# Two stages and a mixture of experts on one core: key spread shared with SP, smaller routing batches, earlier overlap

## What is computed

```python
# own: attention within each sequence (8 heads of 64, one shared key/value head, three branches, gated)
x1 = layernorm(x + attn(x))
# cross: 16 heads of 8 over the context, 64 keys for each sequence
q = x1 @ Wq + bq;  k = ctx @ Wk + bk;  v = ctx @ Wv + bv
r = x1 + softmax(q_h @ k_h.T / sqrt(8)) @ v_h @ Wo + bo
x2 = layernorm(r)
# experts: 8 of them, the two best of each row
t = rmsnorm(x2) * norm_scale
logits = t @ gate_w + gate_b
w = softmax(top2(logits))
y = sum(w[e] * (swiglu(t @ mlp1_w[e] + mlp1_b[e]) @ mlp2_w[e] + mlp2_b[e]) for e in top2)
out = layernorm(x2 + y)
```

## Time and profile before

| what | value |
|---|---|
| three runs | 630.25, 633.15 and 634.72 us, median 633.15 |
| the profiled execution | 630.97 us |
| its span, first to last instruction | 629.0 us |
| busy: TensorE, VectorE, ScalarE, GpSimd | 82%, 76%, 69%, 69% of the span |
| granted clock of TensorE, mean | 0.93 of full speed |

### The profile page before, as it was taken

One profiled execution on the slowest core, in us unless ns is written; L12 is line 12 of the kernel. 1 busy time (PEld: TensorE's weight loads), 2 busy tenths in 40 slices (PEclk: granted clock), 3 DMA queues, 4 the chain that ended last, 5 costly groups with the idle time before them and its releaser, 6 DMA issues.

```text
span 629.0 us, 17434 instructions
## 1 busy us (share of the span) xinstructions
PE 517.8 (82%) x5258; PEld 405.9 (65%) x5258; DVE 478.0 (76%) x1705; ACT 432.9 (69%) x1295; POOL 435.2 (69%) x446
## 2 busy tenths in 40 slices
PE   6678888888888789999999997457677888998862
PEld 3456666666666656777767765447567888887720
DVE  3679999999998776888997896646566468897602
ACT  3789999999998768888977763225334445667703
POOL 6678889898896672665668988673566654687622
PEclk9889999999998999999999998576779889999976
DMA  2256565654542221111111111231122221623152
GB/s 71 63 209 225 213 254 194 240 167 116 160 143 63 57 72 36 44 46 42 40 37 44 40 40 53 53 94 42 50 68 61 67 64 43 208 70 85 50 168 67
DMA packets 71503, 60.69 MB, mean 96 GB/s; under 512 B 21592, under 2 KB 64758, under 8 KB 69110
## 3 DMA queue, kind: packets, MB, share of 16 engines
q1 hardware_dynamic: 66230, 50.03, 26.4%
q0 software_dynamic: 4608, 8.50, 4.1%
q10 hardware_dynamic: 576, 1.05, 0.5%
HBM read 28.50 MB, written 32.08 MB: 96 GB/s over the span
## 4 chain that ended last, share of the span: by engine, by line
PE 43%; DVE 19%; ACT 14%; issue 13%; another core or an unknown queue 5%; POOL 3%; DMA 2%; DVEq 0%; SPq 0%; ACTq 0%; POOLq 0%
ACT l_weights L394 8%; PE ps L1496 5%; PE ps L1476 5%; PE ps L882 4%; PE ps L964 4%; PE ps L871 3%; PE ps L348 3%; PE ps L325 2%; PE ps L337 2%; PE ps L916 2%; PE ps L909 1%; DVE l_shifted L1165 1%; DVE a_ms L527 1%; PE ps L355 1%
## 5 line engine op out<-in xcount | busy, mean ns | idle before, releaser
L1630 POOL DMA_INDIRECT y_dram<-l_keys,l_blk x80 | 80.3, 1003 | 64.5 <-ACT l_keys L1568 41.4
L394 ACT ACTIVATE l_weights<-ps,a_nb,a_rinv 128x64 f32<-128x64 f32 x256 | 99.5, 413 | 3.4 <-DVE a_nb L517 1.7
L817 POOL DMA_INDIRECT disp_dram<-l_R,x_pos x64 | 64.6, 1009 | 17.6 <-issue 17.6
L1074 POOL TENSOR_TENSOR l_keys<-x_kT,l_table 128x1024 f32<-128x1024 f32 x32 | 61.3, 1919 | 4.5 <-PE ps L882 4.5
L483 POOL TENSOR_TENSOR a_rinv<-a_ms,a_halfneg 128x10 f32<-128x10 f32 (+1 forms) x32 | 62.2, 1943 | 2.8 <-DVE a_ms L527 2.0
L1496 PE MATMUL ps<-l_table,l_keys 128*128 x320 | 49.6, 303 | 10.9 <-ACT l_keys L1581 6.3
L394 ACT ACTIVATION_READ_ACCUMULATOR l_weights<-ps,a_nb,a_rinv 128x1 f32 x256 | 54.7, 214 | 0.0
L1496 PEld LDWEIGHTS ps<-l_table,l_keys 128*128 128x128 f32 x320 | 43.1, 209 | 16.4 <-issue 16.1
L1712 DVE TENSOR_SCALAR l_work<-ps 128x512 f32<-128x512 f32 x40 | 27.5, 688 | 34.1 <-PE ps L1476 18.5
L1568 ACT ACTIVATE l_keys<-ps,l_blk 128x128 f32<-128x128 f32 x80 | 25.0, 364 | 40.2 <-PE ps L1496 24.5
L1142 DVE TENSOR_REDUCE x_mx<-ps 128x16 f32<-128x1024 f32 x32 | 39.1, 1222 | 15.0 <-PE ps L882 14.9
(11 more groups left out here) (235 smaller groups left out, 1676.7 us busy)
## 6 DMA issues: line engine op xcount, KB each, us to landing
disp_dram<-l_R SPq DMA_DIRECT2D x16, 1048.0 KB, 4.3
l_blk<-disp_dram SPq DMA_DIRECT2D x80, 65.5 KB
l_shifted<-in_xT SPq DMA_DIRECT2D x32, 64.0 KB, 2.0
l_R<-in_x SPq DMA_DIRECT2D x32, 64.0 KB, 1.9
l_W1h<-v_dram SPq DMA_DIRECT2D x64, 32.0 KB, 2.5
x_dram<-a_xo SPq DMA_DIRECT2D x32, 64.0 KB, 1.8
l_W1l<-in_w SPq DMA_DIRECT2D x4, 512.0 KB
x_xa<-x_dram SPq DMA_DIRECT2D x32, 64.0 KB, 1.8
```

The source lines that it names most:

```text
L394: last = nc.scalar.activation(E[:, e.u4, g, :], ps_Sh[:, g % 2, g // 2, 0:D], ACT.Exp, bias=nb[:, e.u2, g:g + 1], scale=rinv[:, e.u4, g:g ...
L817: nc.gpsimd.indirect_dma_start(out=disp[:, :], out_offset=bass.IndirectOffsetOnAxis(ap=pos[:, B, k_, j:j + 1], axis=0), in_=R[:, t, k_, :] ...
L1074: G.tensor_tensor(KB[:, c.t % 3, :, :, :], kT[:, c.u4, :].rearrange("p (b k) -> p b k", b=2).unsqueeze(2).to_broadcast([P, 2, 8, T]), hm[: ...
L1630: G_.indirect_dma_start(out=Y[:, :], out_offset=bass.IndirectOffsetOnAxis(ap=blk[:, (2 * q + j) % NB, PLACE:PLACE + 1].bitcast(I32), axis= ...
```

## The change

1. The cross stage starts one step sooner: OFFSET 34 to 33, in SP's stream (OFFSET - 3) 31 to 30.
2. The key spread is split. The key buffer's layout is turned so that a head place's two sequences lie side by side (128 columns, 512 bytes). GpSimd fills the first 4 of 8 places of both 64-partition halves (512 columns). For the others SP copies rows straight from the keys, 8 transfers a tile (8 partitions by 512 bytes each) at lag 5 of its stream; VectorE clears those places once, at step 1. TensorE's scores (lag 5) and ScalarE's reuse of a key buffer wait for the transfers.
3. The logits come out of the output product: gate weights, less their column mean and multiplied by the output weights, stand as 8 more columns (GATED = 136) of `wo`, x1 times them is added in (12 buffers of turned x1), and VectorE scales by the row's power at lag 11. The turning of rows (L921), ScalarE's copy (L1022) and the old product (L958) go. The weights are made once, in steps 1 to 8.
4. Batches are of 4 tiles throughout, eight of them, and each phase comes two steps sooner. Their ranks use fp32 counts. Scatters start at step 20 and not 26: two a step up to step 35, one a step in 36 to 41, the rest (from row 38) between pairs.
5. The table of part 0 is made over steps 32 to 35, that of part 1 at step 49.
6. Pairs start behind step 38 (WEAVE 44 to 39): pair n shares the streams with step 39 + n. For steps from 39 on the turned output and the output product use another PSUM bank.
7. xb has 8 buffers and not 4.

```diff
-OWN_LAG, CROSS_LAG, OFFSET = 10, 28, 34
-WEAVE = 44
+OWN_LAG, CROSS_LAG, OFFSET = 10, 28, 33
+WEAVE = 39
+GATED = P + 8
...
-    BATCHES = ((0, 8), (8, 8), (16, 4), (20, 4), (24, 4), (28, 4))
+    BATCHES = tuple((t, 4) for t in range(0, tiles, 4))
...
-        placed_rows = 2 * sum(n for t, n in BATCHES if step >= t + n + 18)
-        some = min(placed_rows - sent, 2 if step < tiles + 3 else 3) if step < tiles + 10 else 0
+        placed_rows = 2 * sum(n for t, n in BATCHES if step >= t + n + 16)
+        some = min(placed_rows - sent, 2 if step < tiles + 4 else 1) if step < tiles + 10 else 0
...
+            if v.live:
+                if v.t == 0:
+                    sp.wait_ge(later.cleared, 10)
+                v.wait(sp, k_ready)
+                v.free(sp, scored, 3)
+                for g in range(2):
+                    for c in range(HALF, 8):
+                        s = slice(T * g + D * c, T * g + D * c + D)
+                        sp.dma_start(KB[s, v.t % 3, c, :, :].rearrange("p q k -> p (q k)"), kT[s, v.u4, :]
+                                     ).then_inc(keys_in[v.t % 3], 16)
...
-                h.free(sp, y_added, 4)
+                h.free(sp, y_added, 8)
...
+                nc.tensor.matmul(ps_y[:, P:GATED], x1T[:, k.t % 12, :], gw[:, :], start=False, stop=False,
+                                 skip_group_check=True)
                 nc.tensor.matmul(ps_y, oT[:, k.u2, :], wo[:, :], start=False, stop=True,
                                  skip_group_check=True).then_inc(y_done, 1)
...
                 d.wait(pe, k_spread)
+                pe.wait_ge(*keys_landed(d.t))
...
-            if m.live:
-                m.wait(pe, row_ready)
-                m.free(pe, tT_ready, 1)
-                nc.tensor.transpose(ps_t, R[:, m.t, 0, 0:P], idf[:, :]).then_inc(t_turned, 1)
...
-            if o.live:
-                if o.t == 0:
-                    pe.wait_ge(prepared, 1)
-                o.wait(pe, tT_ready)
-                nc.tensor.matmul(ps_lg, tT[:, o.u2, :], gw[:, :], start=True, stop=True).then_inc(logits, 1)
...
-            if m.live:
-                m.wait(act, t_turned)
-                m.free(act, logits, 2)
-                nc.scalar.activation(tT[:, m.u2, :], ps_t, ACT.Copy).then_inc(tT_ready, 1)
...
                 G.tensor_tensor(
-                    KB[:, c.t % 3, :, :, :],
-                    kT[:, c.u4, :].rearrange("p (b k) -> p b k", b=2).unsqueeze(2).to_broadcast([P, 2, 8, T]),
-                    hm[:, :].unsqueeze(1).unsqueeze(3).to_broadcast([P, 2, 8, T]),
+                    KB[:, c.t % 3, 0:HALF, :, :].rearrange("p c q k -> p c (q k)"),
+                    kT[:, c.u4, :].unsqueeze(1).to_broadcast([P, HALF, P]),
+                    hm[:, 0:HALF].unsqueeze(2).to_broadcast([P, HALF, P]),
                     ALU.mult).then_inc(k_spread, 1)
...
-            if o.live:
-                o.wait(dve, logits)
-                oB = batch_of[o.t]
-                V.tensor_tensor(lg[:, oB % 2, o.t - BATCHES[oB][0], :], ps_lg, later.gb[:, :],
-                                ALU.add).then_inc(lg_kept, 1)
...
+                V.scalar_tensor_tensor(lg[:, lB % 2, l.t - BATCHES[lB][0], :], r[:, l.u2, P:GATED],
+                                       later.rs[:, l.t, 1:2], later.gb[:, :], ALU.mult, ALU.add).then_inc(lg_kept, 1)
...
+                V.memset(KB[:, :, HALF:8, :, :], 0.0).then_inc(later.cleared, 1)
```

More of the change, by code:

```diff
@@ L971, in tally @@
             pe.wait_ge(counted, B + 1)
-            nc.tensor.matmul(ps_cnt, later.onesb[:, :], cum[:, B + part, :], start=True, stop=True).then_inc(tallied, 1)
+            nc.tensor.matmul(ps_cnt, ones32[:, :], cum[:, B + part, :], start=True, stop=True).then_inc(tallied, 1)
         return slot, lambda: None
@@ L1177, in slot @@
                 n.upto(mark[0])
-                mark[0] = n.add(V.reciprocal(v_(p1), v_(d1)))
+                mark[0] = n.add(V.reciprocal(weight(0), v_(d1)))
             if rank:
@@ L1198, in slot @@
                 n.upto(mark[0])
[L1199 removed]
+                mark[0] = n.add(V.tensor_tensor(weight(1), weight(0), v_(e2), ALU.mult))
             if k.live:
@@ L1255, in slot @@
                 V.tensor_tensor(Brest[:, 1, :], Brest[:, 0, :], Bpart[:, 1, :], ALU.subtract).then_inc(B_rest, 1)
-            if step_of(at) == tiles + 6:
-                table(0)
-            if step_of(at) == tiles + 19:
-                table(1)
+            if TALLY < step_of(at) <= TALLY + 4:
+                table(0, step_of(at) - TALLY)
+            if step_of(at) == tiles + 17:
+                for phase_ in range(1, 5):
+                    table(1, phase_)
         def count(part):
@@ new lines, in table @@
+            if phase_ == 2:
+                n.add(V.tensor_tensor_scan(cend[:, :], one8[:, :], nb[:, :], 0.0, ALU.mult, ALU.add))
+                n.add(V.tensor_scalar(wr[:, :], nb[:, :], -float(P), float(cap), ALU.mult, ALU.add))
+                n.add(V.tensor_scalar(first_row[:, :], later.blocks[0:1, :], float(P), float(LISTS[part]), ALU.mult, ALU.add))
+            if phase_ == 3:
+                n.add(V.tensor_tensor(past[:, :, :], cend[0:1, :].unsqueeze(1).to_broadcast([1, NB, 8]),
+                                      later.blocks[0:1, :].unsqueeze(2).to_broadcast([1, NB, 8]), ALU.is_le))
+                n.settle()
+                n.add(V.tensor_tensor(wm[:, :, :], past[:, :, :], wr[0:1, :].unsqueeze(1).to_broadcast([1, NB, 8]), ALU.mult))
+                n.add(V.tensor_reduce(er[:, 0, :], past[:, :, :], AX.X, ALU.add))
@@ L1297, in vector, with double @@
+        def double(part):
+            t = slice(PARTS[part][0], PARTS[part][0] + PARTS[part][1])
+            dve.wait_ge(ln_rstd, PARTS[part][0] + PARTS[part][1])
+            n.add(V.reciprocal(later.c2[:, t], later.rs[:, t, 1]))
+            n.settle()
+            n.add(V.scalar_tensor_tensor(later.c2[:, t], later.rs[:, t, 0], 2.0, later.c2[:, t], ALU.mult, ALU.mult))
         later.double = double
@@ L1458, in begin @@
             load_experts(0)
+            later.bank_free(pe)
             turn_rows(0)
-            pe.wait_ge(later.tT_ready, tiles)
             turn_rows(1)
@@ L1710, in pair @@
                 return
+            if p == PA // 2:
+                later.double(1)
             dve.wait_ge(up, p + 1)
```

202 lines of the change are left out of this document (121 added, 81 removed).

## The result

The changed kernel took 687.35 us (median of four runs, 678.93 to 688.23) against 631.8 us for the kernel before beside it (median of four): a ratio of 1.084, 95% interval 1.075 to 1.094. The forecast was 618 us, range 598 to 636. It is slower, outside the range, and of the cases it is the one that was given 8%: SP sets the step.

The account below looks back on a forecast made before the run. Bounds by stretch: TensorE, VectorE, then GpSimd in the cross steps, nothing full in steps 36 to 43, unexplained waits in early pairs. -2 - 1.7 - 17.3 + 8 = -13 from 630.97 gave 618 us, range 598 to 636.

Parts of the forecast that it names:

- SP sets the step: Rival, 8%: at 0.62 us an issue SP needs 6.1 us a cross step against 4.9; +38, 656 us.
- the price of SP's issue: SP's eight new key transfers a step: 0.33 us each, taken from three issues of the same shape.
- Cross a step sooner: Before step 10: one step fewer in which both stages run; -2 us, bounds 0 to -4.9.
- Key spread 0.95: GpSimd's key spread in the cross steps, halved: from 1.90 to 0.95 us.
- Steps 10 to 36: Cross steps 10 to 36, summed by stretch: -1.7 us together, bounds -6 and +5.
- GpSimd's bound gone: Stretch 327.7 to 379.5 us: GpSimd no longer bounds, TensorE's 4.9 us a step replaces 5.18; -2.7 us.
- batches of four: VectorE, steps 15 to 46: eight batches, not six, 22 small ops each at 0.13 us; 0.7 us a step.
- Pairs from step 39: Step 36 to the first clamp: 19.5 us instead of 36.8; -17.3 us, bounds -22 and -10.
- What comes back: Pairs 0 to 19: steps 39 to 43 now run between pairs 0 and 4; +8 us, bounds 0 and +18.
- light steps: Rival, 15%: steps inside the pairs cost 13.3 us instead of 8, plus three waits of about 1.8; +10.5, 628 us.
- more batches: Rival, 7%: VectorE +1.0 us a step over 22 steps and +18 in the pairs; about 637 us.
- run freely: Rival, 20%: first twenty pairs lose 18 of 24 us of unexplained waits; 600 us.

Follow-up runs that it names:

- b_sbuf: Kernel before plus eight unused SP transfers per cross step, 8 rows by 512 bytes, SBUF to SBUF: 696.07 us, ratio 1.100.
- b_dram: Kernel before plus eight unused SP transfers per cross step, same shape, loaded from device memory to SBUF: 639.11 us, ratio 1.009.
- b_dram_plain: Kernel before plus eight unused device-memory loads per cross step, compiled with `nc.dge_precook = False` around their loop: 654.15 us, ratio 1.103.
- a_half6: Changed kernel with GpSimd filling six head places instead of four, SP making four transfers a tile instead of eight: 641.76 us, ratio 1.015.
- a_half8: Changed kernel without SP's eight transfers a tile; GpSimd fills all eight head places: 648.04 us, ratio 1.027.
- a4_all2: Changed kernel with keys through device memory, pairs from step 41, two scatters a step in steps 36 to 41: 629.85 us, ratio 0.998.
- a6_same: Same kernel as a_half6, rerun as reference on a chip of the second kind: 609.65 us, ratio 1.030.
- a6_w41: Changed kernel with six head places by GpSimd and pairs from step 41 instead of 39: 599.67 us, ratio 1.014.

## Why the prediction was wrong

*The step that failed* is the price of SP's issue: "I take 0.33, the same shape", against the 0.62 of the v spread that stood beside it as the upper bound. The shape was the wrong likeness. b_sbuf, b_dram and b_dram_plain show the same shape at 0.625, 0.295 and 0.623 us. The v spread's price (median 0.61 in the trace of before) was the near one; what the two have in common no trace shows. With 0.667 a piece, gap included, and 1.5 for the others (forecast 1.1), SP's step is 6.85 us, and the forecast's own threshold of 0.48 an issue is passed.

*The rival "SP sets the step"* had the mechanism, and its chance of 8% was far too small for two rows of SP's own queue that differed by two. Its 656 was low by 31 us. It allowed 38 us for the steps, at 6.1 us of SP a step and not 6.85; measured against the forecast's own terms, 17.2 came before step 10 and 40.9 behind it, 58 together, of which some 11 are not SP's (a_half6's +9.7 behind step 10 against the forecast's -1.7). The remaining 11 us lie in the start of the pairs and in pairs 0 to 19, where it inherited the forecast. What stood against it, that issues don't wait for landings, agrees with 0.295 us an issue in b_dram and with the v spread in the trace of before (0.61 an issue, a median of 2.5 us to its landing), and proved nothing about the price of an issue.

*Cross a step sooner, -2.* Not shown. Where SP's issues don't set the step, step 10 comes at 242.2 (a_half8), 243.2 (a4_all2) and 245.4 (a_half6) on chips of the first kind, against 244.8 and 243.1 in the kernel before.

*Key spread 0.95.* It was 1.12. Half of the columns is not half of the time: 1024, 768 and 512 columns took 1.92 to 1.96, 1.52 to 1.57 and 1.12 on average.

*Steps 10 to 36, -1.7 with bounds -6 and +5.* Wrong also without SP: +9.7 in a_half6, +17.1 in a_half8, +8.5 in a4_all2. The term "GpSimd's bound gone, -2.7" asked what GpSimd no longer does; VectorE, at 118 of 135 us busy, was the engine that got the work (127.9 in a_half6), and two scatters a step now stand before each power from step 20 and not 26. The sum charged batches of four on six steps alone. Its 0.13 an operation was about right (9.5 us for 67 more), its reach was not. Nor did TensorE's step get shorter: the product of 8 columns costs 0.24 us in each of 52 records where the old one cost 0.22, the output product 0.32 where it was 0.30, and TensorE's busy time rose from 131.1 to 135.1 us. That VectorE's work is what lengthens the steps is argued from these numbers and stays open.

*Pairs from step 39, -17.3.* -15.0 in the changed kernel, -15.8 and -16.8 in a_half8 and a_half6, well inside its bounds. Right.

*What comes back, +8 with bounds 0 and +18.* +16.8. The forecast priced the steps that run inside. On chips of the second kind they show in the first three gaps between clamps: 19.9 us in a6_same against 11.7 in the schedule of before (b_dram_plain), 8.2, which looks like the forecast. On the kind that was measured they don't: before took 19.2 us for these three gaps, the kernel after 21.1, so +1.8. The fourth gap went from 10.2 to 16.3 us, +6.1 (it is 4.0 in a6_same), and the sixteen behind it add 8.9. Missing is the other half: the forecast called GpSimd's scatters gone ("one a step now"), though they were only put later, behind powers that wait for VectorE. a6_w41, with pairs from step 41, takes 14 us of the pairs' time away on the second kind.

*The rivals "light steps" and "more batches".* The first (15%) put pairs 0 to 19 at +18.5, close to the measured +16.8, but by steps that cost more inside, and on this kind of chip the gaps that hold them grew by 1.8. The second (7%) had the right complaint about VectorE; its own terms, 22 us and 10 above the forecast, come to some 650 and not to its 637.

*The rival "run freely"*: no. The pieces that no engine's work explains didn't shrink, they grew, from 24 us before the twentieth pair to 34. The chain of waits in the kernel after, its two longest, to be read beside the earlier trace rows (start, length):

```profile
480.88 12.16 another core or an unknown queue
...
545.98 6.25 another core or an unknown queue
```

What is known of them is told in the last section.

## What to carry to other kernels

Don't price a DMA issue by its shape: 8 rows of 512 bytes cost 0.295 us an issue in b_dram and 0.625 in b_sbuf. The two memories are not enough either: the v spread comes from device memory, as the loads at 0.295 us do, and costs 0.61, and one compile setting takes the same load from 0.295 to 0.623. Where no trace shows the very transfer, put it into the kernel before and read its price there, as b_sbuf does. Where two rows of one queue differ by a factor of two, and the queue fits into the step with the cheap one and not with the dear one, the dear one is the forecast's main case until something excludes it. Add up the step of a queue that only issues as that of an engine: SP's came to 6.85 us here, and no engine was full. When work is moved ahead of a stage, list what each engine's stream then holds in front of the next stage's feed; here it was GpSimd's scatters behind powers behind VectorE.

## What the runs showed of the hardware

**Two kinds of chip.** The kernel before takes 632 us on one kind and 592 on the other. One kernel was traced on both (a_half6 and a6_same, 641.76 and 609.65 us): 24 of the 32 us lie in pairs 0 to 19 (121.4 and 97.3), 4 in pairs 20 to 39, 3 in steps 10 to 36. On the first kind TensorE's answers (the increments of its semaphores, on which the other engines wait) come late while GpSimd sends scatters without a pause. In the kernel after, the products of pairs 12 and 13 and what waits for them:

```profile
530.34 0.98 POOL L1694 DMA_INDIRECT y_dram<-l_keys,l_blk  x1 [3.20 <-ACT l_keys L1632]
...
534.15 0.78 PE L1540 MATMUL ps<-l_W1h,m_th 128*128 x2
...
536.43 0.63 PE L1540 MATMUL ps<-l_W1h,m_tl 128*128 x2
...
538.04 0.96 POOL L829 DMA_INDIRECT disp_dram<-l_R,x_pos  x1 [0.31 <-issue]
...
538.61 0.48 PE L1540 MATMUL ps<-l_W1h,m_th 128*128 x2
...
540.35 0.60 ACT L1624 ACTIVATE l_weights<-ps 128x512 f32<-128x512 f32 x1 [4.96 <-PE ps L1540]
...
540.35 0.69 DVE L1778 TENSOR_SCALAR l_work<-ps 128x512 f32<-128x512 f32 x1 [6.27 <-PE ps L1540]
...
542.23 0.99 POOL L1694 DMA_INDIRECT y_dram<-l_keys,l_blk  x1 [3.23 <-ACT l_keys L1632]
```

Pair 12's last product starts at 536.43, but both ScalarE and VectorE get on only at 540.35, 3.3 us after its end, at the time at which pair 13's semaphore increment appears too. GpSimd's run of seven scatters, begun at 530.34, ended at 539.00. It then waits until the released work feeds it (542.23), and the pattern repeats every 11.9 us: behind the four runs of seven between 506 and 551 and the run of six after them, the silence of TensorE's increments ended 1.2 to 1.4 us after the last scatter, each time. The longest silence, 15.1 us up to 493.04, ended 2.1 us behind the run of fourteen. It is not a full stop: one to three increments do appear within each of these runs. On the second kind of chip (b_dram_plain) an answer comes in the middle of such a run:

```profile
500.57 1.00 POOL L1639 DMA_INDIRECT y_dram<-l_keys,l_blk  x1 [0.30 <-ACT l_keys L1577]
...
501.85 0.40 PE L1485 MATMUL ps<-l_W1h,m_tl 128*128 x2
...
501.87 0.99 POOL L1639 DMA_INDIRECT y_dram<-l_keys,l_blk  x1 [0.30 <-issue]
...
502.28 0.60 ACT L1569 ACTIVATE l_weights<-ps 128x512 f32<-128x512 f32 x1 [0.87 <-PE ps L1485]
...
503.16 0.96 POOL L818 DMA_INDIRECT disp_dram<-l_R,x_pos  x1 [0.30 <-issue]
```

On that kind a6_same shows 61 scatters without a pause and never more than 3.9 us without an increment. The lengths and prices of the scatters are the same on both (1.0 us and 0.3 of gap). This is a coincidence in time, seen in each trace of the changed schedule on the first kind (the longest silence before pair 20: 10.6 us in a_half8 and 11.3 in a_half6, ended 2.2 us behind a run of fourteen scatters, and 10.0 in a4_all2, ended 1.4 us behind a run of seven); that the scatters are its cause was not shown, because the runs without them all fell on the second kind. The silences lie where the chain of waits names "another core or an unknown queue", the 12.16 us piece (480.88 to 493.04) above all.

**An SP issue's price doubled under `nc.dge_precook = False`**: 0.295 us in b_dram, 0.623 in b_dram_plain, at the same shape, source and size.
